# Stages 0 to 2 of a four-stage attention kernel: the order in which each engine's steps are merged

## The reference

```python
x = _L0_xattn_ref(x, ctx_2048, ...)   # chan: attention over channels; softmax(q k) applied to v, + x
x = _L1_xattn_ref(x, ctx_2048, mask_1x1xSxS2_fc1, mask_Bx1xSxS2_ff1, ...)
    # layernorm, self attention (16 heads of 16, masked), + x
    # layernorm, cross attention on ctx_2048 (16 heads), + x
    # layernorm, MLP 256 -> 1024 -> 256 with gelu, + x
x = _L2_xattn_ref(ctx_2048, x, mask_BxS2_ik0, ...)
    # lat: x attends to ctx_2048 and itself (256 keys, 16 heads), + x
    # rmsnorm, MLP 256 -> 1024 -> 256 with gelu, + x of the stage's start
x = _L3_xattn_ref(x, ctx_2048, ctx_2048, ...)   # two cross attentions, 16 heads of 128, and an MLP
```

## Time and profile before

| | us |
|---|---|
| median of three runs (lowest, highest) | 2092.71 (2091.19, 2097.3) |
| the profiled execution | 2088.43 |
| its span from the first to the last instruction | 2086.7 |
| PE busy in the span | 1932.1 |
| DVE, ACT, POOL busy | 1275.4, 1183.9, 678.1 |
| stages 0 to 2 (PE until stage 3's stretch begins) | about 935 |
| stage 3 | about 1152 |

### The profile page before, as it was taken

One profiled execution on the slowest core, in us unless ns is written; L12 is line 12 of the kernel. 1 busy time (PEld: TensorE's weight loads), 2 busy tenths in 40 slices (PEclk: granted clock), 3 DMA queues, 4 the chain that ended last, 5 costly groups with the idle time before them and its releaser, 6 DMA issues.

```text
span 2086.7 us, 43191 instructions
## 1 busy us (share of the span) xinstructions
PE 1932.1 (93%) x14880; PEld 1677.8 (80%) x14880; DVE 1275.4 (61%) x4143; ACT 1183.9 (57%) x3879; POOL 678.1 (32%) x613
## 2 busy tenths in 40 slices
PE   5679899999999999888999999999899999999889
PEld 3457678787777777667999999999799999999878
DVE  4668897978787875454555555556455555555663
ACT  3377787878787877436444444443644444444631
POOL 1233444444444443423222222132322222222462
PEclk7899999999999999999999999999999999999999
DMA  7000000000000000000000000000000000000100
GB/s 264 8 9 7 7 12 2 11 4 4 4 4 4 2 2 1 22 24 28 20 26 15 25 20 15 25 16 26 19 19 26 15 25 20 15 20 0 41 11 31
DMA packets 24635, 44.35 MB, mean 21 GB/s; under 512 B 2336, under 2 KB 12064, under 8 KB 23584
## 3 DMA queue, kind: packets, MB, share of 16 engines
q1 hardware_dynamic: 24336, 42.19, 6.2%
q10 hardware_dynamic: 144, 0.20, 0.0%
HBM read 40.28 MB, written 2.10 MB: 20 GB/s over the span
## 4 chain that ended last, share of the span: by engine, by line
PE 48%; DVE 2%; ACT 2%; issue 1%; POOL 1%; ACTq 0%; DVEq 0%; POOLq 0%
PE general L1965 32%; PE o_psum L2022 6%; PE scores L2004 5%; PE pT_psum L2081 3%; PE scores L2131 1%; ACT probs L1636 1%; POOL probs L1540 1%; PE o_psum L2131 1%; PE pT_psum L2131 1%; PE general L1976 0%; DVE oT L1807 0%; ACT oT L1652 0%; DVE guess L1317 0%; DVE row_stats L1769 0%; DVE totals L1798 0%
## 5 line engine op out<-in xcount | busy, mean ns | idle before, releaser
L567 POOL TENSOR_TENSOR probs<-probs,rsums 128x512 f32<-128x512 f32 (+1 forms) x288 | 283.8, 999 | 470.2 <-DVE rsums L794 469.6
L1540 POOL TENSOR_TENSOR probs<-probs,rsums 128x512 f32<-128x512 f32 x128 | 133.4, 1042 | 733.9 <-DVE rsums L1800 733.9
L617 ACT ACTIVATE probs<-negated,negmax 128x128 f32<-128x128 f32 (+1 forms) x768 | 325.5, 431 | 10.9 <-DVE negmax L785 10.7
L1644 ACT COPY probsT<-pT_psum 128x512 f32<-128x512 f32 x128 | 75.0, 586 | 283.2 <-PE pT_psum L2081 283.2
L1112 PE MATMUL pT_psum<-ident,probs 128*128 128x128 f32 x1072 | 176.3, 286 | 50.9 <-ACT probsT L625 24.1
L1112 PEld LDWEIGHTS pT_psum<-ident,probs 128*128 128x128 f32 x1072 | 123.7, 143 | 106.6 <-ACT probsT L625 43.4
L1965 PE MATMUL general<-hT,w_qk 128*128 128x512 f32 x768 | 206.4, 404 | 1.8 <-ACT kT L1619 1.5
L1965 PE MATMUL general<-w_o,oT 128*128 128x256 f32 x1536 | 197.8, 282 | 1.6 <-ACT oT L1652 0.9
L1965 PE MATMUL general<-ctxT,w_qk 128*128 128x512 f32 x750 | 195.1, 396 | 2.9 <-DVEq L222 2.9
L1965 PEld LDWEIGHTS general<-w_o,oT 128*128 128x128 f32 x1536 | 187.7, 188 | 11.6 <-DVE oT L1807 4.0
L1636 ACT ACTIVATE probs<-scores,negmax 128x128 f32<-128x128 f32 x512 | 180.5, 370 | 23.9 <-DVE negmax L1792 23.9
(11 more groups left out here) (199 smaller groups left out, 3914.2 us busy)
## 6 DMA issues: line engine op xcount, KB each, us to landing
raw_qk<-w_qk_dram SPq DMA_DIRECT2D x32, 256.0 KB, 2.9
weights_a<-weights_a_dram SPq DMA_DIRECT2D x2, 2048.0 KB, 18.1
raw_v<-w_v_dram SPq DMA_DIRECT2D x16, 256.0 KB, 2.7
raw_vrows<-vrows_dram SPq DMA_DIRECT2D x16, 256.0 KB, 3.4
raw_o<-w_o_dram SPq DMA_DIRECT2D x16, 256.0 KB, 2.7
weights_a<-weights_a_dram SPq DMA_DIRECT2D x3, 1024.0 KB, 11.1
ctx_in<-ctx_dram SPq DMA_DIRECT2D x8, 256.0 KB, 2.7
X<-x_dram SPq DMA_DIRECT2D x8, 256.0 KB, 16.1
```

What stands on the lines that cost most here:

```text
L567: nc.gpsimd.tensor_tensor(pr, pr, rsums[:, n % 4, 0:segs].unsqueeze(2).broadcast_to([P, segs, width(kind) // segs]), ALU.mult).then_inc(s[ ...
L617: last = nc.scalar.activation(probs[:, n % PROBS, i * wide:(i + 1) * wide], src[:, i * wide:(i + 1) * wide], ACT.Exp, scale=1.0 if kind == ...
L1540: nc.gpsimd.tensor_tensor(pr, pr, rsums[:, t % 2, :].unsqueeze(2).broadcast_to([P, NB, P]), ALU.mult).then_inc(s["probs_ready"], 1)
```

## The change

The tables of planned times, `by_plan`, `of_units`, `of_names`, `of_last` and `in_order` go. In their place each engine has a string of letters over all eight groups, one letter for each step, and `merged` takes at each letter the next step of that letter's stream. The streams themselves (`BLOCKS_A`, `UNITS`, `WORK_ORDER`, `NORM_ORDER`, `ADD_ORDER`, `LOAD_ORDER`) are written out as lists. The functions that issue a step stay as they are.

The letters are: on TensorE s scores, t turn, v values, w work, f first; on VectorE f front, r rsum, c copy, o values_read, w read, n norm, h first_high, k first_read, z first_norm; on ScalarE e exps, c copy, o values_read, w read, h first_high; on GpSimd p normalise, a add, x mask of cross, y mask of lat, l first_low.

```diff
-PERIOD = 100.0
-SCORES = {('chan', 0): -56.65, ('chan', 2): -53.05, ('self', 0): 2.04, ('self', 4): 11.35, ('cross', 0): 80.21,
-          ('cross', 4): 89.81, ('lat', 0): 224.27, ('lat', 4): 236.69, ('lat', 8): 259.02, ('lat', 12): 270.59}
-AFTER = {'front': {'chan': (5.08, 2.43), 'self': (1.09, 1.75), 'cross': (3.38, 1.5), 'lat': (2.64, 1.01)},
...
-TENSOR_ORDER = in_order([(SCORES[kind, u] + PERIOD * g, "scores", kind, g, u) for kind, g, u in FIRST_UNITS],
-                        of_units("turn", UNITS), of_units("values", FIRST_UNITS),
-                        of_names("work", WORK_ORDER, {name: at for name, (at, _) in WORK.items()}),
-                        [(at + LAST, "first", name, GA - 1, half) for name, ats in FIRST_WORK.items() for half, at in enumerate(ats)])
...
+def merged(letters, **streams):
+
+
+    left = {letter: iter(steps) for letter, steps in streams.items()}
+    order = [next(left[letter]) for letter in letters]
+    assert not any(list(steps) for steps in left.values())
+    return order
...
+TENSOR_STEPS = (
+    "wwwssttvttvwwwswwstwtwtttvttwtvwsswtwttvtsvwwstwwtwswttvttsttwtvtwtwttvtwtstsvwwtwwwtwvtwstwvwwwwwswwtwt"
+    "wwstwtwtvwtsttwvtwtwtstwvtwtstttvwtwttstvwtswtwtsvtwtwtstvtwtvtwtswwtvwwtwstwtwvtwtstwtwvwtwtstwtwvtwtwt"
...
+VECTOR_STEPS = (
+    "ffrrfrfcroconwfffrfrffrfrcfrcrrrccwfnffrfrrrcwcofonfffrrwfffrcfrfrrfcfrfcrfrcfrfrrcfrrrcrcwfcnrwnfffrrrc"
...
+GPSIMD_STEPS = (
+    "pppxxpppppppappyppppappapppyppppxppppppppapppaapppppxpppppppppppppppppppppppppppaappppyaappppppppppppppp"
...
+TENSOR_ORDER = merged(TENSOR_STEPS, s=[("scores", *unit) for unit in FIRST_UNITS], t=[("turn", *unit) for unit in UNITS],
+                      v=[("values", *unit) for unit in FIRST_UNITS], w=steps_of("work", WORK_ORDER),
+                      f=[("first", name, GA - 1, half) for name in FIRST_WORK for half in range(2)])
```

More of the change, by code:

```diff
@@ L109 @@
[L109 to L117, removed]
@@ L121 @@
[L121 to L126, removed]
@@ L127 @@
[L127 to L144, removed]
+NORMS = ("ln1", "ln2", "ln3", "rms")
@@ new lines, with listed, steps_of @@
+KINDS = {"c": "chan", "s": "self", "x": "cross", "l": "lat"}
+def listed(text):
+    return [(name, int(g)) for name, g in (word.split("/") for word in text.split())]
+def merged(letters, **streams):
[3 more added lines that the diff above has]
+    return order
+def steps_of(step, items):
+    return [(step, name, g, 0) for name, g in items]
+BLOCK_WORDS = """
+    c0 c0 s0 s0 c1 c1 x0 x0 s1 s1 c2 c2 x1 x1 s2 s2 l0 l0 c3 c3 l0 l0 x2 x2 s3 s3 l1 l1 c4 c4 l1 l1 x3 x3 s4
+    s4 l2 l2 c5 c5 l2 l2 x4 x4 s5 s5 l3 l3 c6 c6 l3 l3 x5 x5 s6 s6 l4 l4 c7 c7 l4 l4 x6 x6 s7 s7 l5 l5 l5 l5
+    x7 x7 l6 l6 l6 l6 l7 l7 l7 l7
@@ new lines @@
+""")
+NORM_ORDER = listed("""
+    ln1/0 ln2/0 ln1/1 ln3/0 ln2/1 ln1/2 ln3/1 ln2/2 ln1/3 rms/0 ln3/2 ln2/3 ln1/4 rms/1 ln3/3 ln2/4 ln1/5
+    rms/2 ln3/4 ln2/5 ln1/6 rms/3 ln3/5 ln2/6 ln1/7 rms/4 ln3/6 ln2/7 rms/5 ln3/7 rms/6 rms/7
+""")
+ADD_ORDER = listed("""
+    self/0 self/1 cross/0 mlp1/0 self/2 cross/1 mlp1/1 self/3 cross/2 lat/0 mlp2/0 mlp1/2 self/4 cross/3 lat/1
+    mlp2/1 mlp1/3 self/5 cross/4 lat/2 mlp2/2 mlp1/4 self/6 cross/5 lat/3 mlp2/3 mlp1/5 self/7 cross/6 lat/4
+    mlp2/4 mlp1/6 cross/7 lat/5 mlp2/5 mlp1/7 lat/6 mlp2/6 lat/7 mlp2/7
@@ new lines @@
+VECTOR_ORDER = merged(VECTOR_STEPS, f=[("front", *unit) for unit in UNITS], r=[("rsum", *unit) for unit in UNITS],
+                      c=[("copy_dve", *unit) for unit in UNITS if unit[2] % 2 == 1],
+                      o=[("values_read", *unit) for unit in FIRST_UNITS if unit[0] == "chan"],
+                      w=steps_of("read", [item for item in WORK_ORDER if item[0] in VECTOR_READS]), n=steps_of("norm", NORM_ORDER),
+                      h=steps_of("first_high", [(name, GA - 1) for name in FIRST_ROWS]),
+                      k=steps_of("first_read", [(name, GA - 1) for name in FIRST_WORK]), z=[("first_norm", "x", GA - 1, 0)])
@@ new lines @@
+SCALAR_ORDER = merged(SCALAR_STEPS, e=[("exps", *unit) for unit in UNITS], c=[("copy_act", *unit) for unit in UNITS if unit[2] % 2 == 0],
+                      o=[("values_read", *unit) for unit in FIRST_UNITS if unit[0] != "chan"],
+                      w=steps_of("read", [item for item in WORK_ORDER if item[0] not in VECTOR_READS and not item[0].endswith("_down0")]),
+                      h=steps_of("first_high", [(name, GA - 1) for name in FIRST_PARTS]))
+GPSIMD_ORDER = merged(GPSIMD_STEPS, p=[("normalise", *unit) for unit in UNITS], a=steps_of("add", ADD_ORDER),
+                      x=[("mask", "cross", g, 0) for g in range(GA)], y=[("mask", "lat", g, 0) for g in range(GA)],
+                      l=steps_of("first_low", [(name, GA - 1) for name in FIRST_LOW]))
@@ L210, in before @@
+LOAD_ORDER = [("ctx", "chan_k", g, 0) if name == "ctx" else ("mask", name.split("_")[1], g, 0) for name, g in LOAD_WORDS]
 def before(step, names, name, g, order):
```

107 lines of the change are left out of this document (67 added, 40 removed).

## The result

The changed kernel takes 2035.87 us (median of 4 runs, 2035.14 to 2042.55), the one before in the same session 2094.64 (2091.19 to 2097.3). The ratio is 0.9727 (95% interval 0.9701 to 0.9754). It is taken over all runs, not from the two medians, and of 2093 us it is 57 us (the medians lie 58.8 apart). 22 were forecast, and 36 were the most that the range held. The profiled execution took 2035.49 us with a span of 2033.5.

What follows compares the result with a forecast made beforehand. PE, busy 93% of the span, was taken as the bound, with 118.3 us idle before stage 3. Terms −4, −3.5, −8, −3, −9 gave −27.5, less a fifth −22: 2071 us from 2092.71, range 2056 to 2091.

Steps and rivals of the forecast that it cites:

- the start: 0–150 us, 53.8 us of PE idle time: −4 us, bounds +1 and −9.
- the steady periods: 300–750 us, 23.1 us of PE idle time: about −2.2 us a period, taken as −8 (0 to −14).
- the end: 835–935 us, 17.4 us of PE idle time: −9 us (0 to −14), including half of the clock's loss.
- PE's busy time stays, and the sum has only idle time in it: Whole kernel: no instruction, wait, buffer or transfer comes or goes, so only PE's idle time was counted as gain.
- a bare pair: Two turns with under 0.75 us of other PE work between; five fewer in the start at 0.78: −3.9 us.
- From the losses that I can't find one by one I take off a fifth: Whole sum: part of what one wait gives back is taken by the next, so −27.5 became −22 us.
- 0.94 and 0.60 stay: their producers keep their place: Steady periods: PE's waits for rms's norm (0.94 us) and values of lat behind DVE's copy (0.60) would remain.
- What they give is in the steady term: Fewer long DVE two-input fronts beside GpSimd matter only where DVE is late; no separate size given.
- The −1.7: Start: PE's 3.61 us wait at 51.73 shortens because DVE's reciprocal now stands ahead of the front of self.3.
- (1): DVE bounds the front half of the period; only start and end gain: −10, 2083 us; chance 0.12.
- (2): The idle time only moves, each filled pair taking cover from elsewhere: 0, 2092 us; chance 0.11.
- (3): Moved adds and hoisted reciprocals put GpSimd beside DVE's fronts, up to 1.06 us a hit: +9, 2101 us; chance 0.09.

Runs made afterwards that it cites:

- b2: Changed kernel with 32 pairs of turns laid bare in the steady periods, a work moved behind the second turn: 2075.23 us.
- a1 to a3: Kernel before with all four new lists only up to rms/0, between rms/0 and rms/4, or from rms/4 on: 2073.20, 2076.31, 2069.89 us.
- e2: Changed kernel with GpSimd's masks of lat for groups 3 and 6 moved back ahead of the adds of cross and lat: 2041.05 us.
- c3: Kernel before with GpSimd's mask of lat for groups 3 to 7 moved behind the adds and the next normalise: 2096.03 us.
- b4: Changed kernel with GpSimd's old list until rms/4: 2045.01 us.
- d1: All four lists reordered from the changed kernel's by exchanges of neighbours under a model of the waits: 2063.60 us.
- c4: Kernel before with VectorE's reciprocal of self.0/0 moved ahead of the front of self.3/0: 2093.46 us against 2092.19.
- e1: Kernel before with ScalarE's read of chan_q/1 moved behind the copy of self.0/0: 2089.98 us against 2093.55.
- c1: Kernel before with VectorE's read of mlp1_down1/7 moved ahead of two casts and two reciprocals: 2092.67 us against 2093.91.
- a3: Kernel before with all four new lists only from rms/4 on: 2069.89 us against 2092.13.
- a4: Kernel before with GpSimd's new list alone: 2094.43 us against 2092.13.

## Why the prediction was wrong

**The place and the sign were right, the sizes weren't.** That only time ahead of 935 us can be won, that stage 3 stays, that the start, the steady periods and the end each give some and that the sign is negative held. The stretches to rms/0 gave 19.4 for the forecast's 7.5, the four steady periods 14.7 for 8 (of 450 us), the rest 19.7 for 12. Three steps of the prediction failed: a term set to nothing (16.8 us), the waits priced too low (37.2 us of idle time went, the sum had 27.5), and a fifth taken off (5.5). Together they are the 32 us between the forecast's 22 and the 53.8 of the table.

**"PE's busy time stays, and the sum has only idle time in it"** failed, by 16.8 us, and is the largest of the three. Part is the clock. The stretch at half the clock at the end is gone (843.15 to 853.39 at 0.50 in the earlier trace rows, 1.00 throughout the changed kernel's last two stretches), and in the start the mean granted clock rose from 0.85 to 0.88. The other part is that each wait adds to PE's busy time too. In a stream a turn starts while the instruction ahead of it still runs, and adds 0.44 us; behind a wait nothing overlaps, and it adds its whole 0.66. In the kernel before, in a stream:

```profile
834.74 0.38 PE L995 MATMUL general<-weights_a,upT 128*128 128x256 f32 x1
834.95 0.60 PE L1112 MATMUL pT_psum<-ident,probs 128*128 128x128 f32 x4
835.39 3.62 PE L995 MATMUL general<-weights_a,upT 128*128 128x256 f32 x16
```

In the steady periods, at full clock in both kernels, PE's waits of 0.15 us and more fell from 38 to 22 and the busy time by 3.9 us: 0.24 a wait, beside 0.68 of idle time. Over all stretches to stage 3 PE's listed waits fell from 134 to 93; at 0.24 each that is an estimate of 10 us of the 16.8, and some 7 are left for the clock. The trace of before had both turns; the sum priced a bare pair at 0.78, while b2 measured 1.11 in its trace.

**"From the losses that I can't find one by one I take off a fifth"** failed. There was nothing to take off: the three stretches add up to the whole (a1 to a3), and bare pairs cost all of their wait (b2). But without it the sum was 27.5, still half of what was measured.

**"0.94 and 0.60 stay: their producers keep their place"** failed. PE's waits for `xhat_y` in the steady periods, 4.7 us in five, are 0.2 in the changed kernel. A step can keep its place in its engine's list and still run earlier against PE: ahead of the norm of rms/1 DVE stood for 1.04 us, for a turn that it had to copy, and that turn now comes sooner. And one instruction of the norm itself is shorter. L842 (L865 in the changed kernel) ran beside GpSimd's normalises and ended with them:

```profile
399.32 3.04 POOL L567 TENSOR_TENSOR probs<-probs,rsums 128x512 f32<-128x512 f32 x3 [0.96 <-DVE rsums L794]
401.49 0.89 DVE L842 SCALAR_TENSOR_TENSOR var<-mv,newton 128x2 f32<-128x2 f32 x1
L842 DVE SCALAR_TENSOR_TENSOR var<-mv,newton x8: 160/888/894, 299.9 to 912.0; 128x2 f32<-128x2 f32 x8
L865 DVE SCALAR_TENSOR_TENSOR var<-mv,newton x8: 160/160/162, 281.3 to 858.0; 128x2 f32<-128x2 f32 x8
```

0.73 us less in a norm that PE waits for would take 0.94 down to 0.21, and 0.0 to 0.23 is what PE waits at rms now; no run changes this alone. The wait of 0.60 for the copy of lat.15 went too. e2 shows that adds beside the fronts ahead of it can bring such a wait back, but not that they had made this one: in c3 it stayed, and in groups 2 and 4 of the changed kernel it is gone although their masks still stand ahead of the adds. I read places in lists where I should have followed times.

**"What they give is in the steady term"**, of the port (DVE's long instructions beside GpSimd's), gave it no term of its own, and failed. DVE is busy for 25 us less, 13.7 of it in L785's two-input fronts:

```profile
L808 DVE CUSTOM_DVE_ANT_0 negated<-masked,madd_self 128x128 f32<-128x128 f32 x256 | 70.3, 326 | 11.6 <-issue 10.4 <-DVE masked L801 1.0
L808 DVE CUSTOM_DVE_ANT_0 negated<-masked,madd_cross 128x128 f32<-128x128 f32 x256 | 67.4, 316 | 11.5 <-issue 10.3 <-DVE masked L801 1.0
```

Before these had 74.4 and 77.0 us, with means of 343 and 353 ns. Of the 512, 27 took over 0.6 us before and 16 do now, and each of these ran beside an instruction of GpSimd. Most of the rest of the 25 us is in the norms: in L842, and in L844 (L867 now), which has one input and took up to 0.98 us, against 0.17. So that one input in SBUF doesn't conflict holds for the fronts of lat, not for all of DVE. Fronts stand ahead of copies on DVE, so a long front is a late copy, and of the 37 us that PE idles less 34 are waits for DVE. Which part of these 34 is the port and which is DVE's order stays open, since the three lists are bound to each other. GpSimd's list alone is 9 us of the 57 (b4), and there the fronts are busy for 6.5 us more. Fewer hits don't suffice: in d1 the fronts have 135.3 us, 2.4 less than in the changed kernel, and it is 27.7 slower.

**The start.** The −1.7 came about (3.61 to 1.70), but not for the reason given: the reciprocal alone gives nothing (c4), ScalarE's read alone takes the wait to 1.20 (e1). The masks cost what was said, a little more: the turn of chan.3/0 at 20.02 us (19.4 forecast), ln1/0 0.88 late (0.3 forecast):

```profile
20.02 0.66 PE L1135 MATMUL pT_psum<-ident,probs 128*128 128x128 f32 x2 [1.94 <-POOL probs L590]
```

**The end.** The read of mlp1_down1/7 alone gives nothing (c1). In the new list the casts are also spread between the copies, which is likely why PE no longer waits there; no run tries that alone. The whole end gives 20 to 22 (a3).

**The rivals.** (1) DVE as the bound: its front half was the right place to look, with the wrong sign; it had less to do, not more. (2) The idle time only moves: wrong for the whole, right for a single step (c1). The Trainium skill, "Perfetto Trace Analysis", section "Optimization Strategy", says that such regular bubbles can mean too little PSUM for the next tile. Here the order was another cure: with the single bank kept, the waits at turns for the copies fell from 46.2 to 27.5 us. What a second bank would give wasn't tried. (3) The port hits of the moved adds: the mechanism is real and costs what was said, 1.07 us for a hit (e2), but the new lists have fewer of them, and GpSimd's moves beside the old lists cost 2 to 4 us (a4, c3).

## What to carry to other kernels

When steps are only reordered, count PE's time behind each wait as well as the wait, and don't discount a sum of local waits without a row that shows the loss. Follow times, not places in a list: an engine whose neighbours run sooner runs sooner itself. A move that is good beside one set of lists can cost beside another, so the lists of all engines have to be found together, with the port's collisions counted, and judged by stretches cut at the same steps.

## What the runs showed of the hardware

A turn of four transposes adds 0.44 us to PE's busy time in a stream and 0.66 right behind a wait, at full granted clock. A two-input instruction of DVE of 0.28 us took 1.35 us beside an add of 1.32 us on GpSimd (e2), and 0.28 when that add ended before it. Such an add, 1.3 us later against the front than in the changed kernel, was worth 1 us of PE's time. Of the norms' instructions that write `var`, 20 of 37 took over 0.3 us in the kernel before, and all 20 ended within 0.12 us of an instruction of GpSimd's; none of the 17 short ones ran beside one. The granted clock at the end fell to 0.50 behind a stand of 1.96 us in the kernel before and of 3.9 in c1, and stayed full up to stage 3 where the longest was 0.9 (a3, the changed kernel). But a wait's length alone doesn't decide it: behind the same waits of 0.68 and 0.94 us at rms/4 it was 0.50 for 3.4 us in the kernel before (from 710.0) and 1.00 in c4.
